# Moving the high halves of the attention probabilities from GpSimdE and ScalarE to ScalarE alone, and all low halves to VectorE

## What is computed

```python
q = (text_hidden @ Wq)...          # 16 heads
k = (vision_tokens @ Wk)...; v = (vision_tokens @ Wv)...   # 8 kv heads, each for 2 query heads
scores = jnp.einsum('bhtd,bhsd->bhts', q, k) / scale
scores = jnp.where(mask, scores, -jnp.inf)
attn = jax.nn.softmax(scores, axis=-1)
out = jnp.einsum('bhts,bhsd->bhtd', attn, v)
return out @ Wo
```

## Time and profile before

| | |
|---|---|
| median of 3 runs | 1641.32 us (1639.22 to 1641.51) |
| profiled execution, first to last instruction | 1635.1 us |
| what the median holds beside that span | 6.2 us |
| attention turns, first scores to last projection | from 17.7 us to about 1330 us |
| TensorE busy / VectorE / ScalarE / GpSimdE | 98% / 75% / 51% / 50% |

### The profile page before, as it was taken

How to read it: one execution, slowest core, us unless ns; L and a number is a source line. 1 busy time by engine, 2 the same in 40 slices (tenths; PEclk the granted TensorE clock), 3 DMA queues, 4 the chain that set the end, 5 groups by cost and what they waited for, 6 DMA issues and landing times. The chain is left out here.

```text
span 1635.1 us, 34935 instructions
## 1 busy us (share of the span) xinstructions
PE 1602.2 (98%) x12199; PEld 1150.1 (70%) x12199; DVE 1220.8 (75%) x3512; ACT 829.3 (51%) x2050; POOL 810.2 (50%) x1128
## 2 busy tenths in 40 slices
PE   8999999999999999999999999999999999999994
PEld 5667677777777686777777777777777777665652
DVE  7987676767777676767678778787877766688783
ACT  6764343434344443434344545454454433677783
POOL 3444544536364645445464564646464357444353
PEclk9999999999999999999999999999999999999997
DMA  8753434434334334444344445544444476899984
GB/s 262 179 143 76 88 75 80 97 66 99 70 88 72 88 76 79 83 81 85 66 117 87 97 105 107 107 99 105 98 105 91 97 254 193 257 292 279 301 231 57
DMA packets 395053, 205.69 MB, mean 126 GB/s; under 512 B 347888, under 2 KB 356080, under 8 KB 394880
## 3 DMA queue, kind: packets, MB, share of 16 engines
q1 hardware_dynamic: 380720, 181.32, 45.6%
q0 software_dynamic: 13600, 21.10, 7.0%
q10 hardware_dynamic: 560, 1.05, 0.2%
HBM read 87.67 MB, written 32.41 MB: 73 GB/s over the span
## 5 line engine op out<-in xcount | busy, mean ns | idle before, releaser
L983 ACT ACTIVATE arena<-arena,neg_max 128x256 f32<-128x256 f32 x512 | 253.7, 496 | 378.0 <-DVE neg_max L1300 374.3
L718 POOL TENSOR_SCALAR arena<-arena,prob_scale 128x256 f16<-128x256 f32 x384 | 183.7, 493 | 467.3 <-DVE prob_scale L1309 465.2
L1666 PE MATMUL ps_query<-xn_both,arena 128*128 128x256 f16 x1024 | 279.1, 273 | 0.7 <-DMA xn_both<-xn_half 0.7
L1667 PE MATMUL ps_query<-xn_both,arena 128*128 128x256 f16 x1024 | 279.1, 273 | 0.0
L1668 PE MATMUL ps_query<-xn_both,arena 128*128 128x256 f16 x1024 | 279.1, 273 | 0.0
L1300 DVE CUSTOM_DVE_ANT_0 arena<-ps_score,mask_add 128x256 f32<-128x256 f32 x512 | 186.7, 420 | 120.5 <-PE ps_score L1668 120.5
L1315 DVE SCALAR_TENSOR_TENSOR arena<-arena,prob_scale 128x256 f16<-128x256 f32 x384 | 234.0, 656 | 6.9 <-POOL arena L718 6.9
L1666 PE MATMUL ps_out<-arena,o_t 128*128 128x512 f16 x512 | 194.1, 379 | 0.6 <-DVE o_t L1320 0.5
L1667 PE MATMUL ps_out<-arena,o_t 128*128 128x512 f16 x512 | 194.0, 379 | 0.0
L1668 PE MATMUL ps_out<-arena,o_t 128*128 128x512 f16 x512 | 194.0, 379 | 0.0
L773 POOL DMA_INDIRECT slot_table<-entry,slot_at x128 | 133.2, 1040 | 48.2 <-issue 33.6
(11 more groups left out here) (343 smaller groups left out, 4064.8 us busy)
## 6 DMA issues: line engine op xcount, KB each, us to landing
arena<-w SPq DMA_DIRECT2D x96, 512.0 KB, 7.0
x_in<-x SPq DMA_DIRECT2D x15, 512.0 KB, 3.5
xn_rows<-xn_half SPq DMA_DIRECT2D x15, 512.0 KB, 3.1
out_rows_dram<-x SPq DMA_DIRECT2D x30, 256.0 KB, 2.4
ctx_in<-ctx_t SPq DMA_DIRECT2D x16, 256.0 KB, 3.0
weight_in<-wq SPq DMA_DIRECT2D x8, 512.0 KB, 5.2
weight_in<-wo SPq DMA_DIRECT2D x8, 512.0 KB, 4.6
arena<-arena SPq DMA_TRANSPOSE x256
```

The costliest lines, as they stand in the source:

```text
L718: pool.tensor_scalar(p_rows[:, c, 0, :], probs[:, c, :], prob_scale[:, c:c + 1], 1.0, ALU.mult, ALU.mult).then_inc(norm_hi, 1)
L983: act.activation(probs[:, c, :], probs[:, c, :], ACT.Exp, bias=neg_max[:, c:c + 1], scale=-1.0, accum_out=prob_sum[:, c:c + 1]).then_inc(e ...
L1666: pe.matmul(dst, a.hi, b.hi, start=start and n == 0, stop=False)
L1667: pe.matmul(dst, a.hi, b.lo, start=False, stop=False)
```

## The change

ScalarE writes the high halves of all four cells in one pass (copy with a scale, float32 in, float16 out), where it scaled the last cell before. VectorE writes all four low halves. GpSimdE does nothing for the probabilities. Two semaphores (`last_scaled`, `last_lo`) go. The order of everything else in each queue stays.

```diff
-                    if h == 0:
-                        sp.wait_ge(norm_lo, (CELLS - 1) * i + TB)
-                    else:
-                        sp.wait_ge(norm_lo, (CELLS - 1) * (i + 1))
-                        sp.wait_ge(last_lo, i + 1)
+                    sp.wait_ge(norm_lo, CELLS * i + (h + 1) * TB)
...
-            def probs_high(i):
-                pool.wait_ge(prob_scaled, i + 1)
-                if i:
-                    for h in range(PAIR):
-                        pool.wait_ge(turned[h], 16 * i)
-                for c in range(CELLS - 1):
-                    pool.tensor_scalar(p_rows[:, c, 0, :], probs[:, c, :], prob_scale[:, c:c + 1], 1.0, ALU.mult,
-                                       ALU.mult).then_inc(norm_hi, 1)
-                c = CELLS - 1
-                pool.wait_ge(last_scaled, i + 1)
-                pool.tensor_scalar(p_rows[:, c, 0, :], probs[:, c, :], 1.0, 1.0, ALU.mult, ALU.mult).then_inc(norm_hi, 1)
-                pool.wait_ge(norm_hi, CELLS * (i + 1))
-                pool.tensor_tensor(p_rows[:, c, 1, :], probs[:, c, :], p_rows[:, c, 0, :], ALU.subtract).then_inc(
-                    last_lo, 1)
...
-                probs_high(i)
...
-            def scale_last(i):
+            def probs_high(i):
                 act.wait_ge(prob_scaled, i + 1)
-                c = CELLS - 1
-                act.activation(probs[:, c, :], probs[:, c, :], ACT.Copy, scale=prob_scale[:, c:c + 1]).then_inc(
-                    last_scaled, 1)
+                if i:
+                    for h in range(PAIR):
+                        act.wait_ge(turned[h], 16 * i)
+                for c in range(CELLS):
+                    act.activation(p_rows[:, c, 0, :], probs[:, c, :], ACT.Copy, scale=prob_scale[:, c:c + 1]).then_inc(
+                        norm_hi, 1)
...
-                    probs_low(i, range(CELLS // 2, CELLS - 1))
+                    probs_low(i, range(CELLS // 2, CELLS))
```

More of the change, by code:

```diff
@@ L321, in build @@
         expert_lo = [signal(f"expert_lo{n}") for n in range(3)]
-        value_scaled, masked, maxed, exped, prob_scaled, last_scaled, last_lo = (
-            signal(n) for n in ("value_scaled", "masked", "maxed", "exped", "prob_scaled", "last_scaled", "last_lo"))
+        value_scaled, masked, maxed, exped, prob_scaled = (
+            signal(n) for n in ("value_scaled", "masked", "maxed", "exped", "prob_scaled"))
         x_stats, x_rstd, x_normed = (signal(n) for n in ("x_stats", "x_rstd", "x_normed"))
@@ L1076, in act_program @@
                 if i < TURNS:
-                    scale_last(i)
+                    probs_high(i)
                 if i == 0:
@@ L1292, in maxima @@
                 if i:
-                    dve.wait_ge(norm_lo, (CELLS - 1) * i)
-                    dve.wait_ge(norm_hi, CELLS * i)
-                    dve.wait_ge(last_lo, i)
+                    dve.wait_ge(norm_lo, CELLS * i)
                 for c in range(CELLS):
```

## The result

| | before | changed |
|---|---|---|
| first measurement, median | 1641.41 us (1639.22 to 1642.07, 4 runs) | 1679.62 us (1671.77 to 1684.41, 4 runs) |
| ratio, 95% interval | | 1.0232 [1.0208, 1.0255] |
| span of the profiled execution | 1635.1 us | 1670.0 us (a run of 1671.77) |

The changed kernel came out 2.3% slower; I had forecast 1641.8 us. That is not the last word on it: measured twice more after the experiments, the same program stood at 0.9998 [0.9987, 1.0008] and 1.0001 [0.9988, 1.0015] of the kernel before. Both results need an explanation, and this part gives as much of one as the runs allow.

What follows compares the result with a forecast made beforehand. TensorE bounds the kernel, busy 1602.2 of 1635.1 us. The terms 3.4 + 1.35 - 2.6 - 0.7 - 0.5 - 0.5 gave +0.45 us, moving the median from 1641.3 to 1641.8 us, range 1636.5 to 1649.

Steps and rivals of the forecast that it cites:

- The step that failed: GpSimdE's queue: the change was taken to leave its router DMAs and the expert part untouched; no size was given.
- likeliest case: Whole kernel: no measurable change, 1641.8 us, own range 1638.5 to 1645; chance 0.62.
- Low halves: VectorE, each turn: a fourth low half fits, since pieces take 0.40 us each once GpSimdE leaves the probabilities.
- Rival 1: VectorE's low halves stay slow, delaying scores in 38 short turns: +15 us, 1656 us; chance 0.07.
- ScalarE's copies: ScalarE, each turn: three more copies at 0.40 us, +1.20 us, hidden in a plain short turn; busy time up 190 us.
- j = 4 of blocks 9 to 14: Six turns where xn_high stands between the copies and query_high: scores 0.57 us later, +3.4 us in all.
- Turn 0: First turn: later query_high and query_low delay turn 1's scores by 1.0 us, with VectorE's extra piece +1.35 us.
- Transposes: TensorE's seven waits for transposed probabilities: low halves finish sooner, giving back 2.6 us (0 to 3.3).
- Turns 9 and 122: Two TensorE stalls behind late GpSimdE work vanish: -0.7 us in turn 9, -0.5 us in turn 122.
- The smaller ones: Smaller stalls of scores behind GpSimdE work vanish: -0.5 us, an estimate.
- Around the span: Outside the profiled span: 6.2 us lie around it and stay, giving the median of 1641.3 us before the change.
- Rival 2: GpSimdE's normalisations lie over VectorE's low halves in j = 1 and 3 and hold them: +9 us, 1651 us; chance 0.12.

Runs made afterwards that it cites:

- pace_record: Changed kernel, with GpSimdE waiting for the scaled probabilities only ahead of the second four scatters (j = 0): 1638.20 us, 0.9978 of the kernel before.
- pace_not0: Changed kernel, with GpSimdE waiting for the scaled probabilities in all turns but j = 0, eight scatters still in one run: 1671.86 us, 1.0181.
- before_run_8: Kernel before the change, with its second four scatters moved ahead of GpSimdE's probabilities in j = 0, making a run of eight: 1684.55 us, 1.029.
- the control: Changed kernel, nothing edited, measured again on two later occasions: 1635.06 us, 0.9998, and 1635.70 us, 1.0001 of the kernel before.
- pace_xn_late: pace_record, with ScalarE's next-block x high halves (j = 4) moved behind key_high: 1634.16 us, 0.9945 of the kernel before.
- best: Changed kernel with a wait until four scatters landed, xn_high behind key_high, and turn 0's copies of cells 2 and 3 later: 1629.90 us, 0.9973; again 1630.88, 0.9982.
- run_6: Changed kernel, with the wait for scaled probabilities placed so that scatters run as six and two: 1649.22 us, 1.0080 of the kernel before.

## Why the prediction was wrong, and where it was right

**The step that failed** is the sentence "Its router DMAs and the expert part are not touched". The instructions weren't; their spacing was. I removed an instruction that waits (`probs_high`, for `prob_scaled`) and asked who would miss its result, and not what its wait held back in its own queue. Behind it stood four scatters, ahead of it four more, and without it they became one run. The rows that show it, four scatters, the probabilities at 277.32, four scatters, were in the trace that I had. This is shown by `pace_record` against `pace_not0` (the wait in the right place, 33.7 us) and by `before_run_8` (the loss made in the old kernel, in one run). My own sign of being wrong, a short turn other than j = 4 that starts its scores late, stood in the profile at j = 0. That a run of eight would hurt could not be read from those rows: no run above four was there. But I gave the change of spacing no bound and no rival, so my upper end was 1649 and the result 1679.62. The loss also needs the condition, of which I knew nothing; where it was absent the kernel came out at 1635.06 against 1635.22, by the ratio inside my likeliest case.

**The sum, term by term**, from the traces of the control, where it can be seen undisturbed (stalls by starts):

- *Low halves.* Forecast 0.40 us apart and a mean near 475 ns; measured 492 in the control (222.0 us for 512). Right. Rival 1 needed over 530.
- *ScalarE's copies.* Four take 1.69 us as one group (from 267.37 in the first trace), 0.40 apart. Right. Its busy time grew by 132.6 us (829.3 to 961.9) and not by my 190: I multiplied drawn durations, which overlap; three more steps of 0.40 in 128 turns are 154, and the copies' own group did grow by 152.7 (64.0 to 216.7). Where the other 20 went I did not trace.
- *j = 4 of blocks 9 to 14.* Forecast 0.57 us in six turns; measured 0.51 in six turns, 3.1 in all. Mechanism and place right, shown by `pace_xn_late`.
- *Turn 0.* Forecast +1.35. The scores of turn 1 stall 2.13 us where it was 1.20, +0.93; I had 1.0 for this part. Block 0 as a whole takes 1.1 us longer (from the first scores of turn 0 to those of turn 8). That this is near my sum is luck. In both controls the granted clock of TensorE stands at 0.50 for 3.4 us from just behind that stall (in the second from 26.32 us on), which costs 1.6 us and hides the later waits of the block; my term knew nothing of it. In the kernels with smaller scatters, which are the same program up to there and have no such stretch, block 0 takes 0.5 to 1.3 us longer. `best` brings the stall down to 1.34.
- *Transposes.* Forecast -2.6. Seven waits with 2.2 us became 5 with 1.7 and 4 with 1.0 in the two controls: -0.8 to -1.7 with 0.16 for each wait that went. But those that went in block 0 are in its 1.1 us already; in blocks 9 to 15 the stalls by starts change by 0.0 and -0.6 us. This is the term that was most over-sized: most transposes in those blocks come late without GpSimdE's pieces too.
- *Turns 9 and 122.* Forecast -0.7 and -0.5; both stalls are gone (0.70 and 0.48). Right, though in turn 122 of the controls TensorE now waits 0.7 and 0.4 us for a transpose. The smaller ones: three stalls of 0.24 at scores are gone, 0.7 where I had 0.5.
- Together: +3.1 + 1.1 - 0.7 - 0.5 - 0.7 = +2.3 us, and with the transposes of blocks 9 to 15 +2.3 and +1.7, where I had +0.45. The ratios, 0.9998 and 1.0001, can't tell that from nothing, and neither can the spans: what follows the attention turns took from 288 to 295 us in the twenty traces. So the likeliest case held in the controls, but its sum is no closer than about 2 us.

**Around the span** I put 6.2 us, the median less the span of a trace that wasn't one of the three runs. Profiled runs with a time of their own show 1.8 us (1671.77 less 1670.0). The other 4.4 us are the distance between that execution and those three. They need not be from one occasion: the trace of before has its landings recorded like the later ones, and the kernel before itself measured 1641.41 and 1641.37 us at first and 1634.68 to 1636.73 on the later occasions. The 6.2 does not enter the sum, but I called it a part of the kernel and it is none.

**Rival 2** is not borne out. With the condition absent the normalisations run over the low halves in j = 1 and 3 and no stall appears there. The Trainium skill ("SBUF — State Buffer", section "SBUF: two separate sides") gives the shared port pair to the first comer for the whole instruction; by the low halves, 656 ns on average beside GpSimdE's pieces and 491 without them, the two engines do get in each other's way, as it says, but no low half was held for the rest of a 2.07 us normalisation: in the second control the 112 that lie over one take 519 ns on average, the 400 others 484, and the longest of all 0.86 us.

**What stays open** is the condition. What the runs show: semaphore increments of TensorE late by up to 5.1 us in kernels with the change and 7.2 in `before_run_8`, and matmuls that pause singly; the more scatters stand in a run the later, with a loss from six on; and only on occasions on which the records of landings are incomplete. A candidate, argued and not tested: the recording of events itself. The Trainium skill ("NOTIFIC — the notification-queue block", section "7.1 Overflow: three behaviours, one of which stalls the engine") says that the block which writes such records always backpressures its producers when its internal queues fill, and may so throttle an engine; each scatter adds 16 increments and 32 packets to be recorded at a time when all engines are busy, and it is the scatters' increments that are missing. Against it: by the same page's "10. Constraints, capacities, measured rates" records cost the engine nothing, measured at 6.6 million a second. That rate doesn't cover this case: the first measurement's trace holds 34,680 instructions and 16,331 increments in 1670 us, 30 million a second without the transfers' packets. Missing records may as well be a consequence as a sign of the cause. No run here had the recording off for certain, so none decides. The runs would have been better spent had the changed kernel stood in every batch: the two batches with the condition are just those in which the size of a scatter wasn't tried.

## What to carry to other kernels

An instruction that waits also spaces what stands behind it in its queue. When one is removed, list the DMAs on both sides of it, with their distances before and after, and treat a longer run than the trace has ever shown as an unknown cost with a bound of its own. Here a wait until the first four have landed costs nothing that can be measured (1.0001), on an occasion with the condition, and guards against a 2.3% loss.

Run the changed kernel itself again in every batch, beside what is derived from it. Two kernels with smaller scatters looked like a finding until the unedited one, on the same occasion, showed no loss either.

Moving work to an engine that is half idle is free only in the turns in which nothing else stands there; look for the turn with the extra (here `xn_high`) and move the extra behind what the path needs. The move of the probabilities takes away some stalls and makes others of about the same size; with the others repaired its gain is left. `best` has stalls of 5.0 us in its turns where the kernel before has 7.9, and stands at 0.9973 and 0.9982, which is 0.2 to 0.3%. `pace_xn_late` (0.9945) was never measured beside it, and part of its ratio may be that the kernel before stood at 1641.37 us on that occasion.

## What the hardware showed that was not expected

TensorE can be held up by another engine's transfers with which it shares no data and no semaphore: up to five microseconds between the end of the matmul and its recorded increment in the changed kernel, where in the trace of before the increments of all 1,106 instructions arrive within 0.02 us of the modelled end. The late ones come in bunches: in `run_6` four that were due between 890.49 and 893.75 are recorded at 894.00, 894.12, 894.20 and 894.27.

After some of these stalls the clock of TensorE is lower for a while. At turn 48 of the changed kernel, first measurement:

```profile
552.84 0.37 PE L1647 MATMUL ps_score<-k_both,q_t 128*128 128x256 f16 x1 [3.24 <-issue]
553.01 0.42 PE L1648 MATMUL ps_score<-k_both,q_t 128*128 128x256 f16 x1
553.22 0.42 PE L1649 MATMUL ps_score<-k_both,q_t 128*128 128x256 f16 x1
...
555.35 0.35 PE L1647 MATMUL ps_query<-xn_both,arena 128*128 128x256 f16 x1
555.54 0.27 PE L1648 MATMUL ps_query<-xn_both,arena 128*128 128x256 f16 x1
555.65 0.27 PE L1649 MATMUL ps_query<-xn_both,arena 128*128 128x256 f16 x1
```

After 3.24 us of idling the matmuls start 0.21 us apart and are drawn 0.42 long, twice the usual 0.109 and 0.27: the lower of the two clock levels, 1.2 GHz in place of 2.4. The granted clock is 0.50 from 552.10, still in the idle stretch, to 555.51. A dozen matmuls at double pitch add some 1.2 us to the stall. It doesn't follow each stall: after the 3.20 us of turn 24 the matmuls start 0.11 us apart at once. In the turns of this trace the clock is lower three times, for 3.4 us each (from 26.45, 552.10 and 989.00 us on). That is 4.5 us of the stall totals above, 1.6 of them in block 0.
